# One node window for every two groups of edges in a two-layer graph network

## The reference, cut to what matters

```python
dst = minimum((6250 * uniform((200000,)) ** 2.0).astype(int32), 49999)   # seed 0
_o = argsort(dst, stable=True); src = src[_o]; dst = dst[_o]             # edges in order of destination
# layer 0
msg = relu(x[src] + edge_attr @ W_edge + b_edge)
agg = segment_sum(msg, dst)
h = relu(((1 + eps) * x + agg) @ W1 + b1) @ W2 + b2
h = relu(batch_norm(h));  x = layernorm(x + h)
# layer 1: attention with 4 heads
z = x @ W;  es, ed = z . att_src, z . att_dst          # one number per node and head
e = leaky_relu(es[src] + ed[dst]);  e = where(e == 0, -1000, e)
ex = exp(e - segment_max(e, dst)[dst])
out = segment_sum(ex / segment_sum(ex, dst)[dst] * z[src], dst)
x = layernorm(x + out)
```

## Time and profile before

| | |
|---|---|
| median of 3 runs | 5048.78 us (5046.24 to 5053.94) |
| the profiled execution | 5007.87 us |
| its span (first to last instruction) | 5006.0 us |
| layer 0, 196 groups | about 0 to 2508 us of the span |
| node tables | 2508 to 2586 us |
| layer 1, 196 groups, and the outputs | 2586 to 5006 us |

### The profile page before, as it was taken

One profiled execution on the slowest core, in us unless ns is written; L12 is line 12 of the kernel. 1 busy time (PEld: TensorE's weight loads), 2 busy tenths in 40 slices (PEclk: granted clock), 3 DMA queues, 4 the chain that ended last, 5 costly groups with the idle time before them and its releaser, 6 DMA issues.

```text
span 5006.0 us, 53159 instructions
## 1 busy us (share of the span) xinstructions
PE 3165.6 (63%) x13596; PEld 2405.9 (48%) x13597; DVE 2238.0 (45%) x4481; ACT 789.5 (16%) x1498; POOL 3022.7 (60%) x3229
## 2 busy tenths in 40 slices
PE   6878777887878778777864444444444444444455
PEld 4666655565656555555643333333333333333343
DVE  4333333333333323223355555555555555555566
ACT  2212111211222112112230000010101111111111
POOL 6666656666666556556456666666666666666654
PEclk9898888888888888888887777777777777776677
DMA  4444444444444434334254444444444444444443
GB/s 150 131 132 134 133 124 130 134 127 127 132 130 132 123 122 128 115 120 126 87 157 133 134 135 135 132 133 135 132 134 133 137 128 136 133 132 134 134 131 101
DMA packets 321267, 650.03 MB, mean 130 GB/s; under 512 B 149823, under 2 KB 170537, under 8 KB 321225
## 3 DMA queue, kind: packets, MB, share of 16 engines
q0 software_dynamic: 150272, 413.00, 29.0%
q1 hardware_dynamic: 164681, 230.37, 14.4%
q10 hardware_dynamic: 6272, 6.19, 0.4%
HBM read 636.22 MB, written 13.08 MB: 130 GB/s over the span
## 4 chain that ended last, share of the span: by engine, by line
another core or an unknown queue 36%; PE 20%; issue 19%; DVEq 12%; DVE 9%; ACT 2%; DMA 1%; SPq 0%; POOLq 0%; ACTq 0%
PE psum L1018 7%; PE psum L1029 5%; DVEq L1172 3%; PE psum L681 3%; DVEq L878 2%; DVEq L836 2%; DVE hot_t L869 2%; PE psum L1015 2%; DVE rows L1156 2%; DVEq L874 1%; DVEq L1167 1%; PE psum L1057 1%; DVE acc L1170 1%; PE psum L1038 1%
## 5 line engine op out<-in xcount | busy, mean ns | idle before, releaser
L407 POOL DMA_INDIRECT rows<-in_x,idx x1568 | 1488.4, 949 | 984.8 <-issue 453.1
L407 POOL DMA_INDIRECT rows<-z_tab,idx x1568 | 1496.7, 955 | 890.3 <-issue 466.2
L1156 DVE TENSOR_TENSOR rows<-rows,psum 128x1024 f32<-128x1024 f32 x392 | 474.7, 1220 | 1675.6 <-remote 1100.0
L1018 PE MATMUL psum<-weights,edge_room 128*128 128x256 f32 x3136 | 918.6, 417 | 48.5 <-issue 47.4
L1029 PE MATMUL psum<-rows,onehot 128*128 128x256 f32 x3136 | 853.0, 409 | 125.5 <-issue 121.9
L681 PE MATMUL psum<-rows,onehot 128*128 128x260 f32 x3136 | 911.5, 455 | 0.0
L681 PEld LDWEIGHTS psum<-rows,onehot 128*128 128x128 f32 x3136 | 721.8, 236 | 151.9
L1018 PEld LDWEIGHTS psum<-weights,edge_room 128*128 128x128 f32 x3136 | 666.3, 213 | 244.9 <-issue 90.4
L1029 PEld LDWEIGHTS psum<-rows,onehot 128*128 128x128 f32 x3136 | 624.5, 206 | 251.1 <-issue 172.7
L1102 ACT ACTIVATE rows<-rows 128x1024 f32<-128x1024 f32 x392 | 414.3, 1057 | 1952.0 <-DVE rows L1156 1410.0
L691 PE MATMUL psum<-ident,agg_sb 128*128 128x128 f32 x392 | 105.9, 363 | 657.9 <-ACT agg_sb L770 583.2
(11 more groups left out here) (155 smaller groups left out, 1672.1 us busy)
## 6 DMA issues: line engine op xcount, KB each, us to landing
dst_t<-in_dst_jp SPq DMA_DIRECT2D x197, 512.0 KB
edge_room<-in_edge_t SPq DMA_DIRECT2D x196, 512.0 KB
rows<-in_x,idx POOLq DMA_INDIRECT x1568
rows<-z_tab,idx POOLq DMA_INDIRECT x1568
z_tab<-edge_room SPq DMA_DIRECT2D x14, 455.0 KB, 6.1
idx<-in_src_idx SPq DMA_DIRECT2D x392, 4.0 KB
dst_t<-in_x_t SPq DMA_DIRECT2D x14, 448.0 KB
rows<-in_x_t SPq DMA_DIRECT2D x14, 448.0 KB, 5.0
```

Of the source, the lines that this page charges most:

```text
L407: nc.gpsimd.indirect_dma_start(rows[0:count, u, j, 0:width], None, table, bass.IndirectOffsetOnAxis(ap=idx[0:count, u, j:j + 1], axis=0)). ...
L1018: last = pe.matmul(bank[:, h * D:(h + 1) * D], edge_in[:, u, j * P:(j + 1) * P], w_edge[:, :], start=False, stop=(h == 1))
L1156: dve.tensor_tensor(half, half, psum[:, 2 * b:2 * b + 2, :].rearrange("p b (j d) -> p (b j) d", j=2), ALU.add).then_inc(added, 1)
```

## The change

`first` is now the first destination of every two groups, given to both. The two groups thus share a window: their sums go into one PSUM bank (start on the first product of the even group, stop on the last of the odd one), and copy, turn and add are done once, semaphores counting by 2. In layer 1 the ed window is loaded once for both. The tests on `plan[1]` are as before; `last` is still given per group.

```diff
-        "first": dst_p[::GROUP].reshape(1, GROUPS),
+        "first": dst_p[::2 * GROUP].repeat(2).reshape(1, GROUPS),
...
 (load_ends, layer 1)
+                if u % 2 == 1:
+                    return
                 if not first_round(i):
-                    sp.wait_ge(L.edge_done, g - RING + 1)
+                    sp.wait_ge(L.edge_done, g - 2)
...
-                sp.dma_start(ed_win[:, u, :], ed_parts[bass.ds(base, WIN), :]).then_inc(L.ed_in[u], 16)
+                sp.dma_start(ed_win[:, u // 2, :], ed_parts[bass.ds(base, WIN), :]).then_inc(L.ed_in[u // 2], 16)
...
 (sum_half, layer 0; sum_lagged in layer 1 likewise)
-                    if not early:
-                        pe.wait_ge(layer0.agg_copied, g - 1)
+                    if u % 2 == 0 and not early:
+                        pe.wait_ge(layer0.agg_copied, g - 2)
...
-                    last = pe.matmul(banks[4 + u % 2][:, 0:D], onehot[:, u % 2, j, :], rows[:, u, j, 0:D],
-                                     start=(j == 0), stop=(j == J - 1))
+                    last = pe.matmul(banks[4 + u // 2][:, 0:D], onehot[:, u % 2, j, :], rows[:, u, j, 0:D],
+                                     start=(u % 2 == 0 and j == 0), stop=(u % 2 == 1 and j == J - 1))
...
 (matmul body, layer 0)
-                if n >= 3:
-                    turn_window((u - 3) % RING, g - 3, n < 5)
+                if u % 2 == 0 and n >= 4:
+                    turn_window((u - 3) % RING, g - 3)
...
 (ScalarE body, layer 0)
-                if not (first_round(i) and g < 2):
+                if u % 2 == 1 and not (first_round(i) and g < 2):
                     copy_window((u - 2) % RING, g - 2, 2 * g + 1)
...
 (VectorE body, layer 0)
-                if not (first_round(i) and g < 3):
+                if u % 2 == 0 and not first_round(i):
                     add_window((u - 3) % RING, g - 3, 2 * g + 1)
...
 (layer 1, fast: turn_lagged, copy_lagged and finish likewise once for two groups)
```

More of the change, by code:

```diff
@@ L258, in __init__ @@
                 self.spread_hot, self.scored = s("spread_hot"), s("scored")
-                self.ed_in = [s(f"ed_in_{u}_") for u in range(RING)] if n else []
+                self.ed_in = [s(f"ed_in_{u}_") for u in range(2)] if n else []
                 self.dst_in = [s(f"dst_in_{u}_") for u in range(2)] if n else []
@@ L680, in sum_lagged @@
                         pe.wait_ge(L.msg_ready, msgs * g + j // (J // msgs) + 1)
-                    last = pe.matmul(banks[4 + u % 2][0:WIN, 0:width], onehot[:, u % 2, j, :], rows[:, u, j, 0:width],
-                                     start=(j == 0), stop=(j == J - 1))
+                    last = pe.matmul(banks[4 + u // 2][0:WIN, 0:width], onehot[:, u % 2, j, :], rows[:, u, j, 0:width],
+                                     start=(u % 2 == 0 and j == 0), stop=(u % 2 == 1 and j == J - 1))
                 last.then_inc(L.agg_ready, 1)
@@ L687, in turn_lagged @@
                 if not early:
-                    pe.wait_ge(L.group_done, g)
+                    pe.wait_ge(L.group_done, g - 1)
                 pe.sem_inc(passed, 1)
@@ L723, in body @@
                 if fast:
-                    if n >= 2:
-                        turn_lagged(g - 2, n == 2)
+                    if u % 2 == 1 and n >= 3:
+                        turn_lagged(g - 2, first_round(i))
                     if n >= 1:
-                        sum_lagged((u - 1) % RING, g - 1, n < 3)
+                        sum_lagged((u - 1) % RING, g - 1, first_round(i))
                     spread_ed(i, u + 1, g + 1)
@@ L769, in copy_lagged @@
                 act.wait_ge(L.agg_ready, g + 1)
-                act.copy(agg_sb[:, 0:width], banks[4 + u % 2][0:WIN, 0:width]).then_inc(L.agg_copied, 1)
+                act.copy(agg_sb[:, 0:width], banks[4 + u // 2][0:WIN, 0:width]).then_inc(L.agg_copied, 2)
             def extras(g):
@@ L799, in body @@
                     ins.then_inc(L.summed, 1)
-                    if not start and fast:
-                        copy_lagged((u - 1) % RING, g - 1)
+                    if fast:
+                        if u % 2 == 0 and not start:
+                            copy_lagged((u - 1) % RING, g - 1)
                     elif not start:
@@ L953, in body @@
                     make_hot_t(i, u + 1, g + 1)
-                back = 1 + fast
-                if not (first_round(i) and g < back):
-                    finish((u - back) % RING, g - back)
+                if fast:
+                    if u % 2 == 1 and not (first_round(i) and g == 1):
+                        finish((u - 2) % RING, g - 2)
+                elif not (first_round(i) and g == 0):
+                    finish((u - 1) % RING, g - 1)
             if fast and layer == 1:
@@ L1024, in sum_half, with turn_window @@
                     pe.wait_ge(layer0.onehot_ready, g + 1)
-                    if not early:
-                        pe.wait_ge(layer0.agg_copied, g - 1)
+                    if u % 2 == 0 and not early:
+                        pe.wait_ge(layer0.agg_copied, g - 2)
                 pe.wait_ge(layer0.msg_ready, 2 * g + b + 1)
                 for j in range(4 * b, 4 * b + 4):
-                    last = pe.matmul(banks[4 + u % 2][:, 0:D], onehot[:, u % 2, j, :], rows[:, u, j, 0:D],
-                                     start=(j == 0), stop=(j == J - 1))
+                    last = pe.matmul(banks[4 + u // 2][:, 0:D], onehot[:, u % 2, j, :], rows[:, u, j, 0:D],
+                                     start=(u % 2 == 0 and j == 0), stop=(u % 2 == 1 and j == J - 1))
                 return last
-            def turn_window(u, g, early):
+            def turn_window(u, g):
                 pe.wait_ge(layer0.agg_copied, g + 1)
-                if not early:
-                    pe.wait_ge(layer0.group_done, g - 1)
+                pe.wait_ge(layer0.group_done, g - 1)
                 for k in range(HALF):
-                    last = pe.transpose(banks[6 + u % 2][:, k * WIN:(k + 1) * WIN], agg_sb[:, k * P:(k + 1) * P],
+                    last = pe.transpose(banks[6 + u // 2][:, k * WIN:(k + 1) * WIN], agg_sb[:, k * P:(k + 1) * P],
                                         ident[:, :])
```

43 lines of the change are left out of this document (19 added, 24 removed).

## The result

The changed kernel takes 10363.83 us (median of 4 runs, 10339.48 to 10368.51) against 5051.36 us of the kernel before: 2.0495 times as long, 95% interval 2.0433 to 2.0557. The prediction said 10730 us, in 9500 to 12300. The profiled execution took 10339.48 us.

The account below looks back on a forecast made before the run. GpSimd's gathers were taken to pace both layers; the general layers, scoring pass and smaller stages summed to 10641 us, plus 1.9 around the span, scaled by 1.0082 to 10730 us, with 9500 to 12300 us as the 8-in-10 range.

Parts of the forecast that it names:

- The step that decided: Window count: groups 192 and 193 span 130 nodes, giving 2 windows, so both layers leave the one-window path.
- The scoring pass: Between the layers: 98 iterations of 32 gathers at 1.25 us plus a standstill, 48.9 us each, 4792 us.
- The gap: Standstill per scoring iteration: last gather landing, scores, store and index load issue, load landing; 8.9 us.
- Rival 2: Scoring pass dearer, from reads piling up or a recurring 3.4 us wait: 5827 us, total 11770 us; chance 0.20.
- The general layers: Both layers in general form, from gathers, GpSimd waits and stretched gathers: 2599 us for layer 0, 2557 for layer 1.
- The two-input operations: VectorE operations with both inputs in SBUF stretch gathers by 0.35 of their length: 271 us in layer 0, 250 in layer 1.
- rival 4: General layers paced by each group's chain of copy, turn and add, 14 or 16 us a group: about 11700 us; chance 0.10.
- The small stages: Node network after layer 0 155 us, node tables with 32 gathers 138, 14 output chunks at the end 200.
- the scans: Scans and store after the scoring pass: 16 scans, other passes, transfers, clearing and handovers; 200 us, 100 to 350.
- From the profiled execution to the median: Whole kernel: 10643 us as profiled, scaled by 1.0082 to a median of 10730 us.
- Rival 1: Both layers: shared window really used, each pair saving a copy, a turn and an add: about 4980 us; chance 0.05.
- rival 3: Gathers run freer: no 3.4 us waits in general passes, no stretching, shorter scoring gap: about 9200 us; chance 0.15.

Follow-up runs that it names:

- the host line alone: Kernel before with only `first` shared by two groups, every copy, turn, add and load unchanged: 9672.71 us against 4085.13, ratio 2.367.
- the open tests: Kernel before with `first` shared by two groups and `single` and `mode` accepting a window count of 2: 4094.92 us, ratio 1.0025; again 4100.22, 1.0029.
- the two edits on SBUF inputs: Kernel before with layer 0's one-hot, or layer 1's two weightings, reading SBUF instead of PSUM: 5066.15 us (1.0031) and 5066.32 us (1.0020).

## Why the prediction was right

**The path.** The step that decided, 130 >> 7 = 1, held: the host line alone doubles the time, the open tests undo it, and so does a layout whose widest pair is 125. None of it could be read from the trace before; it took the data and the test on them.

**The scoring pass.** 3136 gathers at 1.254 us were right to 0.5% (0.954 + 0.30). The gap was 7.0 us and not 8.9, 186 us over 98 iterations. Its four parts were taken as 2.8, 1.6, 1.1 and 3.4 us and are, in the lines above, 2.0 from GpSimd's end to the scores, 1.0 for the scores, 1.5 to the second index load and 2.35 from there to the gather: three too long and one too short. With the slightly dearer gathers the stage came out 153 us lower, half of the 304 by which the sum was too high. Rival 2 (a dearer gather, or the 3.4 us wait within the iteration) did not come.

**The general layers.** They lie within 1.4% and 6.4%, but layer 0 with two errors that cancel. The two-input operations were priced at 0.35 of their length, from one instance in the earlier trace rows; alone they take 0.30 and 0.31, and layer 1 came out at 226 us for 250. That the price was near is luck in part, since one instance can't show a mean that runs from nothing to 0.8. In layer 0 they took 125 us for 271, 0.16 of their length. That isn't because most of them are the shorter bias additions: with the host line alone, on the faster kind of chip, the same general pass with the same operations has gathers of 1085 ns, 212 us above the 1488.2 us with open tests on the same chip, or 0.28 of their length. Why the gathers meet them less badly where GpSimd has the long waits stays open. Against that, GpSimd waited 522.5 us for the group's end (L898) where I had carried over 324.5 from before. It looks like rival 4, the chain as the pace, but the chain by itself is not enough: with the host line alone, on the faster kind of chip, the same general pass has 0.6 us of these waits. They go with that kind of chip, as those of the earlier trace rows do, and are longer, as at 1525.63 us above (6.47 for 3.4). That a ring place is now freed only when its group has been added would explain the length; it was not tried.

**The small stages.** Predicted and measured are 155 and 153, 138 and 146, 200 and 208; the scans were put at 200 us and took 153, of which the 37 us for clearing and handovers were an estimate.

**From the profiled execution to the median.** I scaled by 1.0082, the kernel's own relation before; for the changed kernel it was 10363.83/10339.48 = 1.0024. That is 62 of the 366 us.

**What was wrong.** Rival 1, the case on the other side, had 4980 us for the shared window in use: 1.4% of gain. Where it could be measured it is none. I let a third of TensorE's waits go with half of the turns; on that chip there were only 43.7 us of such waits to begin with. Two slips in the text changed nothing: a distance of 130 is three nodes over the allowed 127, not two; and rival 3's terms (649, 521 and 436 us) come to about 9110 us and not 9200.

## What to carry to other kernels

When a kernel chooses its path by a maximum over its data, evaluate that test on the data before pricing any edit: one pair in 98 that is 3 nodes too wide doubled the time, and no view of the profile hints at it. Where one engine's issue sets the pace (here 8 gathers of 1.25 us a group), halving work on the others moves nothing until that pace is broken; then the same edit was worth 2.9%. A price taken from one instance needs the spread of all of them: operations of the same length stretched most gathers by nothing and a few by 1.0 us. A wait removed from a queue may come back elsewhere: of 675 us of index waits removed, 267 were gained.

## What the runs showed of the hardware

The same kernel takes 5050 us on one kind of chip (or in one state of it) and 4085 on another. The waits for an unnamed releaser after every second group (649 us) are absent on the second, and those for TensorE shrink from 206.2 and 97.7 us to 43.7 and 10.1; together 899 of the 919 us between the spans of 5006.0 and 4087.0 (the second span is that of the host line with open tests). TensorE's granted clock differs too (about 0.80 and 0.89). What these waits are was not found. The general pass has them too, there put down to L898: 559.2 us in layer 0 of the changed kernel on the one kind of chip, 0.6 with the host line alone on the other. They also hide what else delays a gather, as the two edits on SBUF inputs show.

A gather's duration depends on its neighbours: 0.95 us alone, the same for rows of 16 bytes (scores) and of 1024 (layer 0); up to 2.0 us beside a two-input operation of VectorE of 1.22 us; 1.94 between SyncE's store and its index load in the scoring pass. The Trainium skill (SBUF — State Buffer, section "Who interferes with whom") has a VectorE instruction with two SBUF inputs block a GpSimd instruction that reads SBUF until it ends, and infers that descriptor generation is not touched; the runs here show an effect on the gathers, in the mean 0.30 of the operation's length and in 105 cases of 1568 about 0.8 of it. These gathers read their indices from SBUF; the runs don't separate that reading from the generating of descriptors.
